# Masked key and value copies on two engines, and a scheduler that reckons with traced lengths

## What is computed

```
x = x + 0.5 * ffn(layernorm(x));  x = x + attn(layernorm(x));  x = x + 0.5 * ffn(layernorm(x))

ffn:  h = rmsnorm(x, gamma1)                      # 16 heads of 16
      q = h @ Wq + bq;  kv = (h @ Wdown + bdown) @ Wup + bup;  k, v = split(kv)
      att = softmax_g(q[t,h] . k[t,g] / 4)        # per token, head against head
      x = x + (att @ v) @ Wo + bo
      h2 = rmsnorm(x, gamma2);  gate = softmax(h2 @ Wg + bg)     # 8 experts
      x = x + sum_e gate[e] * (h2 @ We[e])
attn: q, k, v from x;  softmax_g(q[n,g,:] . k[m,g,:] / 16) over the 8 groups g;  sum over m of p * v
```

## Time and profile before

| | us |
|---|---|
| median of three timed runs | 1081.45 (1079.98 to 1084.95) |
| profiled execution | 1075.92 |
| its span, first to last instruction | 1073.8 |
| mean granted TensorE clock | 0.991 of full speed |
| TensorE busy | 1008.5 (94%) |
| VectorE busy | 864.4 (80%) |
| GpSimd busy | 746.5 (70%) |
| ScalarE busy | 648.4 (60%) |

### The profile page before, as it was taken

How to read it: one execution, slowest core, us unless ns; L and a number is a source line. 1 busy time by engine, 2 the same in 40 slices (tenths; PEclk the granted TensorE clock), 3 DMA queues, 4 the chain that set the end, 5 groups by cost and what they waited for, 6 DMA issues and landing times.

```text
span 1073.8 us, 28494 instructions
## 1 busy us (share of the span) xinstructions
PE 1008.5 (94%) x11320; PEld 782.7 (73%) x11320; DVE 864.4 (80%) x1356; ACT 648.4 (60%) x1347; POOL 746.5 (70%) x743
## 2 busy tenths in 40 slices
PE   4789999999999989999999999877999999999997
PEld 3577888788788776666666666456878788788785
DVE  7888788787877459999999999988877787786852
ACT  4565564565654447777777777557654555655642
POOL 7667476675763449889889889995865574664544
PEclk9899999999999999999999999999999999999999
DMA  6110000000000000000000000000000000000000
GB/s 201 63 49 2 2 2 1 3 1 2 2 2 1 1 2 1 2 2 2 2 2 2 2 2 2 2 2 2 2 21 2 22 4 19 22 1 22 22 1 40
DMA packets 8410, 14.29 MB, mean 13 GB/s; under 512 B 2516, under 2 KB 6102, under 8 KB 8280
## 3 DMA queue, kind: packets, MB, share of 16 engines
q1 hardware_dynamic: 8280, 12.47, 3.5%
HBM read 8.28 MB, written 4.19 MB: 12 GB/s over the span
## 4 chain that ended last, share of the span: by engine, by line
PE 81%; DVE 8%; issue 5%; POOL 3%; ACT 1%; POOLq 0%; DVEq 0%; ACTq 0%
PE psum L448 54%; PE psum L816 5%; PE psum L826 5%; PE psum L842 4%; PE psum L613 3%; PE psum L624 3%; DVE late L1099 3%; DVE oT L1093 2%; PE psum L727 1%; PE psum L742 1%; PE psum L718 1%; PE psum L708 1%; PE psum L664 1%; DVE hT L1085 1%; POOL kvx L1463 1%
## 5 line engine op out<-in xcount | busy, mean ns | idle before, releaser
L448 PE MATMUL psum<-we,h 128*128 128x512 f32 x1536 | 396.6, 402 | 0.3 <-DVE X L1067 0.3
L448 PEld LDWEIGHTS psum<-we,h 128*128 128x128 f32 x1536 | 275.9, 188 | 59.4 <-issue 2.4
L1238 ACT ACTIVATE late<-psum,gate 128x256 f32<-128x256 f32 x256 | 107.2, 471 | 140.9 <-PE psum L448 96.2
L1421 POOL TENSOR_TENSOR late<-late 128x512 f32<-128x512 f32 x64 | 82.5, 1289 | 147.8 <-ACT late L1238 147.8
L1067 DVE SCALAR_TENSOR_TENSOR X<-psum,gate,X 128x256 f32<-128x256 f32 x256 | 122.8, 480 | 60.3 <-PE psum L448 48.3
L1288 ACT ACTIVATE kvx<-psum 128x1024 f32<-128x1024 f32 x128 | 131.3, 1026 | 64.3 <-PE psum L826 64.1
L1093 DVE TENSOR_REDUCE oT<-psum 128x128 fp32r<-128x1024 f32 x128 | 154.6, 1220 | 16.5 <-PE psum L816 16.1
L1099 DVE TENSOR_REDUCE late<-kvx 128x256 f32<-128x2048 f32 x64 | 145.7, 2277 | 0.0
L1463 POOL TENSOR_TENSOR kvx<-kvx,late 128x2048 f32<-128x2048 f32 x32 | 125.7, 3928 | 20.7 <-ACT late L1295 20.7
L1463 POOL TENSOR_TENSOR late<-kvx,late 128x2048 f32<-128x2048 f32 x32 | 125.2, 3914 | 15.8 <-ACT late L1295 15.8
L826 PE MATMUL psum<-oT,neg_id 128*128 128x512 f32 x256 | 89.1, 429 | 15.2 <-DVE oT L1093 14.6
(11 more groups left out here) (153 smaller groups left out, 2010.3 us busy)
## 6 DMA issues: line engine op xcount, KB each, us to landing
X<-in_L_attn_hidden_states SPq DMA_DIRECT2D x8, 512.0 KB, 5.8
out<-X SPq DMA_DIRECT2D x8, 512.0 KB, 2.7
X<-in_L_ffn_We SPq DMA_DIRECT2D x2, 1024.0 KB, 10.6
kvx<-in_L_ffn_Wq SPq DMA_DIRECT2D x1, 256.0 KB, 3.0
kvx<-in_L_ffn_Wup SPq DMA_DIRECT2D x2, 128.0 KB, 3.1
kvx<-in_L_ffn_Wo SPq DMA_DIRECT2D x1, 256.0 KB, 4.2
X<-in_L_attn_Wk SPq DMA_DIRECT2D x1, 256.0 KB, 2.9
X<-in_L_attn_Wq SPq DMA_DIRECT2D x1, 256.0 KB, 3.2
```

Source lines behind the costliest of these rows:

```text
L448: ins = e.matmul(out_ap, l, r, start=(n == 0 and not opened), stop=(n == len(terms) - 1), skip_group_check=opened)
L1238: e.activation(y[:, n // 2 * 2 + w, :], psum[:, u % 3, w * D:(w + 1) * D], ACT.Copy, scale=gate[k % 2][:, i, 2 * n + w:2 * n + w + 1]).the ...
L1421: own.step(e.tensor_tensor(y[:, 0:2, :], y[:, 0:2, :], y[:, 2:4, :], ALU.add))
```

## The change

The eight masked copies of a pair are divided over GpSimd and ScalarE, four each; VectorE has none. The step `expand_V` and its semaphore go. The scheduler gets other numbers: lengths per step, a distance for each pair of engines (`LAG`) instead of 150 ns for all, a time added on TensorE when it passes from wide to narrow matmuls or back (`change`), a bonus for a narrow step behind a narrow one (`SAME`), additions to the rank by the step's name (`SOONER`) and by job (`FIRST`, with job 7 and 15 now among them). The statistics of the second pass and all other instructions are the same; only where they stand in each engine's list differs.

```diff
-EXPAND = "VPAAVPAV"
+EXPAND = "PPAAAPPA"
...
-            put("PE", 440, ("hT", s, p), ("xs", s, p), ("down", s - 1, before), ("q", s - 1, p))
-            put("ACT", 840, ("hT_hi", s, p), ("hT", s, p))
+            put("PE", 435, ("hT", s, p), ("xs", s, p), ("down", s - 1, before), ("q", s - 1, p))
+            put("ACT", 735, ("hT_hi", s, p), ("hT", s, p))
...
-            for w, engine, ns in (("V", "DVE", 1900), ("P", "POOL", 1600), ("A", "ACT", 2150)):
+            for w, engine, ns in (("P", "POOL", 2810), ("A", "ACT", 2540)):
...
+LAG = {"PE": {"ACT": 260, "DVE": 255, "POOL": 300}, "ACT": {"DVE": 140, "PE": 250, "POOL": 180},
+       "DVE": {"ACT": 120, "PE": 140, "POOL": 205}, "POOL": {"ACT": 75, "DVE": 75, "PE": 185, "SP": 0}, "SP": {}}
+NARROW = ("scores", "attend")
+SOONER = {"gateT": 17000, "la_one": 16900, "oT": 9800, "add": 7500, "q_up": 6000, "xs": 4200, "turn_probs": 1100,
+          "gate_sub": 500, "q": 300, "wo": -200, "out_turn": -700, "stats": -1500, "q_zero": -1700, "kv_turn": -8000,
+          "x1_base": -12000, "ysum": -13300, "mult": -31800}
+FIRST = {0: 10000, 1: 10000, 7: 15000}
+SAME = 4000
...
-        rank[p] = steps[p][1] + max((rank[q] + hop for q in follow[p]), default=0)
+        rank[p] = steps[p][1] + max((rank[q] + lag(p, q) for q in follow[p]), default=0)
...
-        if job in (0, 1, B, B + 1):
-            rank[p] += 10000
+        rank[p] += SOONER.get(p[0], 0) + FIRST.get(job % B if job >= 0 else job, 0)
...
-        return steps[p][0] == "POOL" or p[0] in ("half", "split_lo", "expand_V")
+        return steps[p][0] == "POOL" or p[0] in ("half", "split_lo")
...
+    def change(p):
+        narrow = p[0] in NARROW
+        return 0 if steps[p][0] != "PE" or narrow == state["narrow"] else 140 if narrow else 100
...
-        p = max((q for q in ready[engine] if possible(q) <= now), key=lambda q: rank[q])
+        suits = lambda q: SAME if engine == "PE" and state["narrow"] and q[0] in NARROW else 0
+        p = max((q for q in ready[engine] if possible(q) <= now), key=lambda q: rank[q] + suits(q))
...
-        end[p] = now + steps[p][1]
+        end[p] = now + steps[p][1] + change(p)
...
-                elif name == "expand_V":
-                    expand(e, k, "V", lambda o, src, m_: e.tensor_scalar(o, src, m_, None, ALU.mult))
```

More of the change, by code:

```diff
@@ L131, in all_steps @@
+            put("DVE", size(675, 410), ("la_lo", s, w), ("la_hi", s, w))
         for p in range(NT // 2):
             c = 2 * s + p
[L133 to L137 removed]
+            put("PE", 1640, ("q", s, p), ("hT_lo", s, p), ("scores", c - 2), ("split_lo", 1), ("rest_lo", 2))
@@ new lines, in all_steps @@
+            put("DVE", 1390, ("top", c), ("scores", c), ("values", units - 1) if c == 2 * B else None)
+            put("ACT", 520, ("exp", c), ("top", c))
+            put("PE", 435, ("turn_probs", c), ("exp", c), ("attend", c - 1))
+            put("ACT", 1450, ("at", c), ("turn_probs", c))
+            put("PE", 1085, ("attend", c), ("at", c), ("turn_out", c - 1))
+            put("DVE", 1000, ("mult", c), ("attend", c))
+            put("PE", 435, ("turn_out", c), ("mult", c), ("oT", s - 1, p))
@@ L170, in all_steps @@
+            put("ACT", 735, ("h2_hi", s, p), ("h2T", s, p))
+            put("DVE", 785, ("h2_lo", s, p), ("h2_hi", s, p))
         for w in range(split):
@@ L337, in all_orders @@
             left[q] -= 1
-            came[q] = max(came.get(q, 0), end[p] + (hop if steps[q][0] != engine else 0))
+            came[q] = max(came.get(q, 0), end[p] + lag(p, q))
             if not left[q]:
```

136 lines of the change are left out of this document (64 added, 72 removed).

## The result

The changed kernel takes 1065.42 us (median of 1064.62, 1065.42 and 1066.8); a fourth execution, the one profiled first, was disturbed (2441.29 us) and is left out here. Measured again beside the kernel before on one chip it takes 1064.4 us against 1079.27, a ratio of 0.9857 with a 95% interval of 0.982 to 0.9894. So it is faster by 1.4%, about 15 us. The forecast was 1070 us in a range of 1058 to 1081: sign and size were right. Of its three terms two were too small, and the third, for the start of the second pass, lies within what two executions of one order differ by there; so the agreement is partly luck.

The account below looks back on a forecast made before the run. TensorE, busy 94% of the span, was taken as the bound, its idle time mostly at the two pass starts. Terms -5, -3 and -2.7 sum to -10.7 us from 1081.45: 1070.7, said as 1070 us, range 1058 to 1081.

Parts of the forecast that it names:

- The sum: Whole kernel: the three terms give -10.7 us, 1065.2 in the profiled execution's terms, 1070.7 on the timed median's scale.
- the 5.5 us that I added: Whole kernel: the median of the timed runs, 1081.45 us, was taken as 5.5 above the profiled execution.
- The first start: Start of the first feed-forward pass: without VectorE's stretched copies the third scores come sooner; -5 us, bounds -9 and +2.
- 2.1 us lost: VectorE's row in the first pass's start: up-projection low part and statistics go first, so activations start at 14.9, not 12.85.
- The second start: Start of the second feed-forward pass: first `attend` and third scores come sooner in the new order; -3 us, bounds -8 and +3.
- leave this stretch: GpSimd before the second pass: the first job's 2.4 us statistics step moves two normalisations up, out of the last eight normalisations.
- TensorE's sequence: TensorE's narrow matmuls: 15 of 64 blocks joined with another, saving 0.18 us each; -2.7 us, bounds 0 and -4.
- Cost in mid-pass: Feed-forward stages: GpSimd and ScalarE have room and TensorE has experts' products, so the longer copies cost nothing.
- The rival by which the copies become the wait: Both passes: scores wait for the later four-copy queue, 0.74 us a pair, 1095 us for all 32; 9%.
- One of the signs that I had named for being wrong: Among the signs of a wrong forecast: the copies of a pair taking over 4 us from first to last.
- moving work between the two might bring nothing: Rival: VectorE's row at the start and GpSimd's queue cost what the stretching gave; 1083 us, 14%.

Follow-up runs that it names:

- e8: The changed kernel with the gate's separate multiplication by 0.5 on VectorE folded into the multiplication that follows; 1063.66 us, ratio 0.9856 to the kernel before.
- e3: The kernel before, but for the third pair alone VectorE makes no copies (GpSimd four, ScalarE four); 1078.56 us, ratio 0.9986.
- e12: The changed kernel with the gate's 0.5 folded in and, on VectorE, the up-projection weights' split moved behind the first job's low parts; 1062.56 us, ratio 0.9842.
- e1: The changed kernel run again, unedited, beside the kernel before; 1064.40 us, ratio 0.9857.
- e9: The changed kernel without two of its seventeen bonuses by step name, `la_one` and `kv_turn`; 1072.22 us, ratio 0.9935 to the kernel before.
- e6: The changed kernel without the bonuses by step name and without that of jobs 7 and 15; 1078.80 us, ratio 0.9987 to the kernel before.
- e5: The changed kernel without the preference for joining narrow blocks (`SAME` 4000 set to 0); 1067.19 us, ratio 0.9893 to the kernel before.
- e2: The kernel before with VectorE's copies moved to GpSimd and ScalarE, its own order kept on every engine; 1085.96 us, ratio 1.0055.
- e11: The kernel before with VectorE's copies moved, its order kept, and the gate's multiplication by 0.5 folded into the next; 1079.16 us, ratio 1.0001.
- e10: The changed kernel with only `la_one` and `kv_turn` of the bonuses by name, jobs 7 and 15 still favoured; 1078.16 us, ratio 0.9986 to the kernel before.

## Why the prediction was right, and where it was not

**The sum.** Predicted -10.7 us within the profiled execution, and the profiled executions differ by 11.3 (1075.92 and 1064.62). The medians differ by 15: before's profiled execution was near the fastest of its runs (1075.3 to 1086), while after's lie within 1062.8 to 1067.3. So the 5.5 us that I added to come to the median's scale belong to before's spread and not to after. The sum against the profiled time, 1065.2, was nearer.

**The first start, -5.** Measured -7.9 up to the fourth scores, and -6.9 in e8: right in direction, too small, within the bound of -9. The third scores came 6.7 us sooner (5.25 in e8), where 4.2 was forecast. The mechanism holds: no row of VectorE's timeline between 20 and 60 us is over 1.66 us, and that one is four instructions, and e3 shows it alone, 3.7 and 4.5 us at the third and fourth scores. The step that was mis-sized is "2.1 us lost". I took ScalarE's part of the up-projection at 10.43 from before's row, but ScalarE's order had moved too and it was done at 9.51; VectorE's three instructions took 1.9 us and not 2.6. The activations' low parts started at 13.62 and not at 14.9. What was lost is 0.9 us, and e12 shows how: not by VectorE's queue, but by GpSimd's instructions being stretched beside it (in e1 the first of its four copies, 0.99 us for 0.56, and the small one ahead of them, 0.65 for 0.20). The sum also left out the clock, 0.86 before and 1.00 or 0.94 after at 20 to 50 us. What I had as "the order" rests in part on two bonuses (e9).

**The second start, -3.** Measured from `score.64` to `scores.19` +0.9 us in e1, -0.9 in e8 and 0.0 in e12, against a trace of before with the best clock of all; against e3, the same order at 0.93, they are -2.1, -3.9 and -3.0. So the runs show neither a gain of 3 us nor that there is none. What can be told is which steps held. The last normalisation comes 2.9 us later in e1, and 1.9 in e8 and e12, counted from `score.64`, and not 1.2 (the prediction's own pieces, a residual and two copies in and the statistics out, add up to 1.45). The failed step is that the statistics "leave this stretch": from the eighth last normalisation on the stretch is only 0.4 us longer (48.39 us against 47.97), but that normalisation itself starts 2.5 us later behind `score.64`, since GpSimd does the statistics' 2.4 us there instead. Between `score.64` and the last normalisation GpSimd has 3.4 us more to do and as much idle time as before (14.8 us and 14.9). The steps behind it held where the clock did: the first `attend` came 7.3 us behind the last normalisation in e8 and e12 (7 forecast, 10.7 before) and 8.8 in e1; the third scores 12.0, 12.0 and 13.5 (11.2 forecast, 14.8 before). In e1 TensorE was at half clock: 2.17, 2.90 and 1.94 us for blocks that take 1.03, 1.64 and 1.07. e6 shows what the order is worth here: without bonuses this stretch is 6.6 us longer.

**TensorE's sequence, -2.7.** The joined blocks are worth 15 x 0.20 = 3.0 us by the pairs of steps in e5's account, near the term. The two stretches outside the starts became 4.4 us shorter (2.6 and 1.8), in e8 and e12 4.4 and 4.6, a little beyond the bound of -4; so 1.4 us are changes between other kinds of steps, or waits, which I did not count. The two aren't separated.

**Cost in mid-pass, 0.** Right: between 100 and 380 us TensorE's gaps of over 60 ns add up to 0.5 us in both traces, and it is busy 49.92 of 50 us. The rival by which the copies become the wait needed 15 pairs at 0.74 us. From the fifth to the fifteenth pair of each pass the last copy ended at least 1.6 us before its scores began, so there it found none; at the first four it ended 0.3 to 1.2 us before them, at the sixteenth 0.8. One of the signs that I had named for being wrong did come: the copies of nine of the 32 pairs took over 4 us from first to last, up to 6.7, because ScalarE and GpSimd did not begin together. Outside the starts it cost nothing, as TensorE had other work. e2 shows that a near relative of the rival was real: not the copies were late, but the gate's chain, in another order of the same work.

**VectorE beside GpSimd.** In e2 and e11 VectorE's small instructions end within 0.05 us of the GpSimd instruction beside them, after one of it. That agrees with the Trainium skill, "SBUF — State Buffer", section "Who interferes with whom": whoever issues first has the shared pair of ports for a whole instruction, and the other is blocked. At the copies of the earlier trace rows the wait was longer than one instruction: the first of the three copies ran from 40.34 to 47.09, and GpSimd's run without a pause ended at 46.81. By the warning of the Trainium skill in "Perfetto Trace Analysis", section "Optimizing Scalar/DVE Operations", moving work between the two might bring nothing, and for the moved copies alone (e2, +0.55%) that came out; in the forecast it had 14%, with only the argument of one wait against it.

## What to carry to other kernels

Moving work off a contended engine changes which small instructions then lie beside the other engine's, so measure the move with the order kept and with the order made for it: here each half alone was 0.5 and 1.0% slower and both together 1.4% faster. In a list schedule, where a few small steps stand (here a ones part of 0.61 us and a turn, 7.8 us when their bonuses are taken out) can be worth as much as the lengths and distances (7.4 us), though not by themselves (e10). Where one engine has hardly a pause, a piece that is moved ahead within its list is not gone: count from a point ahead of both its places. When an order is followed on one engine, take the other engines' times from their new order too. And before a term of 3 us is called right or wrong, see how much two traces of one order differ in that stretch.

## What the hardware showed that I had not expected

A VectorE instruction on 4 elements in each partition takes 0.18 to 0.22 us alone and 0.74 beside a GpSimd instruction of 0.75. The stretch goes both ways: GpSimd's four normalised copies took 2.18 us in before and e12, and 2.61 in e1 and 3.02 in e8 beside a split on VectorE. TensorE can stand 3.5 us with no semaphore late (e3); in five traces it resumed 1.35 to 1.56 us behind the end of a packet of instructions, which isn't proved to be the cause. The granted clock of one order in one stretch differs between executions: 1.00 and 0.94 at 20 to 50 us for e1 and e8, 0.86 and 0.93 at 700 to 750 for e1 and e8, 1.00 and 0.93 there for before and e3. With it the milestones of a start move by 1.5 us (third scores of e1 and e8) to 3.0 us (before and e3), so a lead at a start is worth reading in two executions.
